# Query projection of two target blocks from f16 parts, with features at a quarter and the weight at four times

## The chip, the cores and the metric

One Trainium2 chip, one of its cores. The time is that of one execution of the whole program on the device, in microseconds (us); where a kernel was run several times the median stands. Engines are named as the profile names them: PE is the matrix engine (TensorE), PEld its weight loads, ACT the scalar engine, DVE the vector engine, POOL the GpSimd engine, SP the engine that issues DMAs.

## The reference

A graph attention layer. 2048 source nodes and 2048 target nodes have 256 features each; 8 heads of 32 features. What is computed, cut to the parts that matter:

```python
hs = layer_norm(h_source, ln1_scale, ln1_bias)
ht = layer_norm(h_target, ln1_scale, ln1_bias)
q = (ht @ Wq + bq).reshape(T, H, HD) / sqrt(HD)
k = (hs @ Wk + bk).reshape(S, H, HD)
v = (hs @ Wv + bv).reshape(S, H, HD)
logits = einsum('thd,shd->hts', q, k)            # masked where edge_mask is 0
ctx = einsum('hts,shd->thd', softmax(logits), v)
ht = layer_norm(ht + ctx @ Wo + bo, ln2_scale, ln2_bias)
return x + ht + gelu(ht @ W1) @ W2
```

The source rows are the rectified, normalized x; the edge mask is the adjacency matrix of 2048 x 2048 integers.

## The kernel before

Targets are worked in four blocks (k = 0 to 3) of 512. Within a block there are 8 units, one for each head (unit u = 8k + r), and within a unit 16 steps, one for each tile of 128 sources. (r, s) below is step s of the unit r of its block.

In each step PE makes the masked scores of the tile that is five steps ahead (`scores`: four mask matmuls of 128 columns and one of 512), a half of an `early_scores` pair (512 columns, for the row maxima of a later unit) and the context of the present tile (eight matmuls of 65 columns). ACT takes the exponential of the scores into one of 8 slots. The low part of the probabilities (exact value minus its 16-bit high part) is made by POOL for 12 of the 16 tiles and by DVE for 4. DVE also takes the row maxima of each early pair, `maxima`. Two early banks alternate, so PE can write pair e only when the maxima of pair e - 2 are done; two score banks alternate, so PE can write the scores of tile n only when the exponential of tile n - 2 is done. At the start of a unit PE waits until ACT has written the row of maxima for its scores (`row_out`), and until ACT has copied the context of the unit before (`context_out`).

Everything else is put by hand between these steps, in the order of each engine's own loop: tables at the top of the file say at which (r, s) or (u, s) a piece is issued. A piece stands in its engine's queue and holds up what comes behind it. The tables that matter here:

- `QT_AT`: at (3, 5) and (3, 11) PE transposes the normalized targets of the next block, and one step later ACT turns them into features (`query_features`) in `cT`, in f32.
- `QP_AT`: at (4, 1), (4, 2) and again at (4, 11), (4, 12) PE makes the queries of the next block, `queries(k, m, c)`: for each half m of the query columns one f32 product of 512 columns for each half c of the features. The trace shows each f32 product as two matmul records. The result is read by ACT (`query_high`) two steps after the start and by DVE (`query_low`) three steps after.
- `T_HIGH`, `T_LOW`: the same features are split into two f16 parts, high by ACT (`feature_high`), low by POOL (`feature_low`), for the residual term of the output rows (`out_row`), where an identity matrix `ident16` adds them. For the next block they stand at (4, 6), (4, 8) on ACT and (4, 11), (4, 14) on POOL.
- `MASK_DVE`: six of eight masks of the next block made by DVE, the last at (4, 7), where the second number counts pairs of steps.
- `HIGH_AT`, `LOW_AT`: W1 and W2 are split into f16 parts in eight pieces each, the high ones by ACT at step 6 of units 3, 4, 5, 6, 7, 12, 13, 14, the low ones by POOL (`weight_low`) at step 12 of units 4, 5, 6, 7, 13, 14, 15, 21.
- `WO_HIGH`, `WO_LOW`: the same for Wo, at (3, 2) on ACT and (4, 5) on POOL (`output_low`), both in block 0.
- At step (4, 1) of blocks 1 and up ACT takes a square root (`row_deviation`), which needs another activation table, and then goes back to the exponential's.

After the last unit comes the feed-forward part: PE makes `up_products` for 8 pieces of each block, ACT takes the gelu of each (`gelus`), DVE the low part, and PE makes `down_products`. The first gelu needs its own activation table.

Of the kernel before, what the change touches and what calls it, by code (L numbers as in the profile page):

```python
# [13 lines left out]
P = 128  # L14
# [6 lines left out]
DC = D // P  # L21
# [25 lines left out]
PLACE = 3 * 16  # L47


WIDE, UNREAD, UNREAD_LATER = 64, 20, 24  # L50
# [14 lines left out]

MASK_DVE = {(2, 3): 1, (2, 6): 2, (3, 2): 3, (3, 7): 4, (4, 3): 5, (4, 7): 6}

# [26 lines left out]
HIGH_AT = [3, 4, 5, 6, 7, 12, 13, 14]  # L94
LOW_AT = [4, 5, 6, 7, 13, 14, 15, 21]

# [98 lines left out]
def gnn_kernel(nc, x, adj, nodemask, h_target, ln1_scale, ln1_bias, Wq, bq, Wk, bk, Wv, bv, Wo, bo,  # L195
               ln2_scale, ln2_bias, W1, W2, out):
    with ExitStack() as top:
# [29 lines left out]
        nidentb = sb("nidentb", [P, P], BF16)  # L227
        ident16 = sb("ident16", [P, P], F16)
        ones16 = sb("ones16", [P, P], F16)
# [7 lines left out]
        node_b = sb("node_b", [P, NT], BF16)  # L237
        cols = sb("cols", [P, 10, DC], F32)
        big = sb("big", [P, 3], F32)
# [10 lines left out]

        LN1_G, LN1_B, BK, BQ, BO, BV, LN2_G, LN2_B, RES_B, Q_B = (cols[:, i, :] for i in range(10))
        std_z, rstd_z, neg_z, neg_x = (col_z[:, i, :] for i in range(4))
# [81 lines left out]
        q_hi = sem("q_hi")  # L334
        t_hi, t_lo, c_hi, c_lo, wo_hi, wo_lo = sem("t_hi"), sem("t_lo"), sem("c_hi"), sem("c_lo"), sem("wo_hi"), sem("wo_lo")
        w_in, w_hi, w_lo = [sem(f"w_in{i}") for i in range(2)], sem("w_hi"), sem("w_lo")
# [63 lines left out]
        with nc.Block() as block:  # L400
# [111 lines left out]
            def _(pe):  # L512
# [134 lines left out]
                def shift_row(u):  # L647
                    pe.wait_ge(shift_ready, u + 1)
                    if u == 0:

                        value_read(pe, 5)
                    aux_free(("shift", u))
                    for t in range(TT):
                        last = mm(aux[0:SHIFT_ROW + 1, t * P:(t + 1) * P], shift[:, t, :], ident16[:, :], True, True)
                    last.then_inc(aux_ready, 1)
# [16 lines left out]
                def out_row(k, t):  # L672

                    if t % 2 == 0:
                        aux_free(("wo", k, t // 2))
                    if t == 0:
                        pe.wait_ge(wo_lo, 1)
                        pe.wait_ge(c_lo, DC * (k + 1))
                        pe.wait_ge(t_lo, DC * (k + 1))
                    dst = aux[:, t % 2 * D:(t % 2 + 1) * D]  # L680
                    part = slice(t * P, (t + 1) * P)
                    for c in range(DC):
                        for a, w in ((0, 0), (0, 1), (1, 0)):
                            mm(dst, c_parts[:, a, c, part], wo_parts[:, w, c, :], c == a == w == 0, False, skip_group_check=True)
                    for c in range(DC):
                        for a in range(2):
                            last = mm(dst[:, c * P:(c + 1) * P], t_parts[k % 2][:, a, c, part], ident16[:, :], False,
                                      c == DC - 1 and a == 1, skip_group_check=True)
                    if t % 2 == 1:
                        last.then_inc(aux_ready, 1)  # L690
# [174 lines left out]
            def _(act):  # L865
# [84 lines left out]
                def negated(u):  # L950
                    act.wait_ge(max_done, (u + 1) * PAIRS)
                    if u > 0:

                        act.wait_ge(aux_ready, AUX["shift", u - 1] + 1)
                    else:
                        act.wait_ge(zeroed, 2)
                    nc.scalar.activation(shift[:, :, SHIFT_ROW], half_max[:, u % 2, 1, :], ACT.Copy, scale=-1.0).then_inc(
                        shift_ready, 1)
# [64 lines left out]
                def query_features(k, c):  # L1023
                    job_here("qT", k, c)
                    affine(t_full[k][:, c, :], aux[:, :], LN1_G[:, c:c + 1], RES_B[:, c:c + 1]).then_inc(aux_done, 1)

                def feature_high(k, c):
                    if k == 0:
                        act.wait_ge(nT_done, c + 1)
                    else:  # L1030
                        act.wait_ge(aux_done, AUX["qT", k, c] + 1)
# [97 lines left out]
                for u in range(UNITS):  # L1129
                    k, r = divmod(u, H)  # L1130
                    for s in range(STEPS):
# [10 lines left out]
                        if k == 0 and (r, s) in T_HIGH[0]:  # L1142
                            feature_high(0, T_HIGH[0].index((r, s)))
                        if k + 1 < NTB and (r, s) in T_HIGH[1]:
                            feature_high(k + 1, T_HIGH[1].index((r, s)))
                        if (u, s) == WO_HIGH:
# [375 lines left out]
            def _(pool):  # L1522
# [51 lines left out]
                def weight_low(i):  # L1574
# [20 lines left out]
                nc.gpsimd.memset(dead_w[:, :], DEAD_W).then_inc(made, 1)  # L1595
                for m in (ident32, identb, nidentb, ident16):
                    last = nc.gpsimd.memset(m[:, :], 0.0)
                link(last)
                for m, one in ((identb, 1.0), (ident32, 1.0), (nidentb, -1.0), (ident16, 1.0)):
                    last = nc.gpsimd.affine_select(out=m[:, :], in_=m[:, :], compare_op=ALU.not_equal, fill=one, base=0,  # L1600
# [22 lines left out]
                for u in range(UNITS):  # L1623
                    k, r = divmod(u, H)
                    for m in range(STEPS):
# [6 lines left out]
                        if k == 0 and (r, m) in T_LOW[0]:  # L1632
                            feature_low(0, T_LOW[0].index((r, m)))
                        if k + 1 < NTB and (r, m) in T_LOW[1]:
                            feature_low(k + 1, T_LOW[1].index((r, m)))
                        if k > 0 and (r, m) in C_LOW:
                            context_low(k - 1, C_LOW.index((r, m)))
                        if (u, m) == WO_LOW:
                            output_low()
                        if m == 12 and u in LOW_AT:  # L1640
                            weight_low(LOW_AT.index(u))

# [41 lines left out]
```

## Time and profile before

| what | us |
|---|---|
| median of 3 runs | 683.53 |
| lowest and highest of the 3 | 681.89, 683.69 |
| the profiled execution's own time | 682.28 |
| its span in the trace | 680.3 |
| the 32 units, from about | 66 to 582 |
| feed-forward part, from about | 582 to 680 |

The profiled execution is one more run of the same kernel; its span starts with the first instruction and leaves out 2.0 us around it. Every row of the trace is from this execution. In the timeline views a row is one instruction or several of the same kind merged, with start, duration, engine, line of the kernel, what it writes and reads, how many, and in brackets how long its engine stood idle before it and who ended that. The granted clock of PE was 1.00 in all of the units quoted, which is 2.4 GHz.

### The profile page before, as it was taken

To read this page: it belongs to the slowest core of one execution; us is meant where nothing else is said; L and a number is where in the kernel's file an instruction comes from. 1 tells how busy PE (TensorE), PEld (TensorE's weight loads), DVE (VectorE), ACT (ScalarE), POOL (GpSimd) and SP (SyncE) were. 2 spreads that over 40 slices of the span, in tenths; PEclk is the share of its full clock that TensorE was granted. 3 is DMA by queue.
4 is the path that set the end of the run, shared out by engine and by line. 5 is a ranking of instruction groups with operands and counts; after the bars stand their busy time and mean duration, and the time that the engine had idled before them with its cause. 6 is when DMAs were issued, how large, how long until landed. Compare 5 with 4: busy or idle time off the path is not lost. (4 is left out here: it accounts for less than half of the span.)

```text
span 680.3 us, 20543 instructions
## 1 busy us (share of the span) xinstructions
PE 649.9 (96%) x8402; PEld 464.2 (68%) x8402; DVE 567.2 (83%) x940; ACT 501.5 (74%) x973; POOL 542.4 (80%) x508
## 2 busy tenths in 40 slices
PE   4999999999999999999999999999999999899998
PEld 4556677766777777677777766777777667457767
DVE  5989899999989979888988798899878887595561
ACT  4767687777789858787898686877976788877450
POOL 4565889999999967999999679999997777383430
PEclk9999999999999999999999999999999999999999
DMA  8835512212101011220011112011000000000001
GB/s 290 281 91 151 167 33 64 64 50 63 33 2 34 2 65 63 67 76 2 2 33 33 64 55 57 19 67 59 4 2 1 2 2 2 1 1 32 24 18 54
DMA packets 20797, 36.23 MB, mean 53 GB/s; under 512 B 2752, under 2 KB 13280, under 8 KB 20704
## 3 DMA queue, kind: packets, MB, share of 16 engines
q1 hardware_dynamic: 20704, 34.92, 16.5%
q8 instruction: 66, 1.08, 0.7%
q14 instruction: 27, 0.22, 0.1%
HBM read 26.49 MB, written 2.10 MB: 42 GB/s over the span
## 5 line engine op out<-in xcount | busy, mean ns | idle before, releaser
L1532 POOL TENSOR_TENSOR prob_lo<-prob 128x512 f16<-128x512 f32 x379 | 432.5, 1168 | 45.7 <-ACT prob L945 44.7
L945 ACT ACTIVATE prob<-score 128x512 f32<-128x512 f32 x512 | 303.8, 597 | 110.4 <-PE score L514 102.5
L514 PE MATMUL score<-nidentb,mask_nat 128*128 128x128 bf16 x2048 | 198.3, 219 | 4.2 <-ACT prob L945 1.6
L514 PEld LDWEIGHTS ctx<-v_sb,prob 128*128 128x128 bf16 x2048 | 158.8, 98 | 61.9 <-ACT raw L967 13.8
L514 PE MATMUL early<-kT,qT 96*128 96x512 f16 x512 | 191.8, 380 | 6.7 <-DVE half_max L1316 5.7
L514 PE MATMUL score<-qT,kT 97*128 97x512 f16 x512 | 195.3, 381 | 0.0
L514 PE MATMUL ctx<-v_sb,prob 128*128 128x65 f16 x2048 | 191.5, 193 | 2.9 <-ACT raw L967 2.5
L1316 DVE CUSTOM_DVE_ANT_0 early<-early,mask_nat,half_max 128x1024 f32<-128x1024 f32 x128 | 163.9, 1286 | 33.3 <-PE early L514 31.7
L514 PE MATMUL ctx<-v_sb,prob_lo 128*128 128x65 f16 x2048 | 190.4, 193 | 0.0
L514 PEld LDWEIGHTS ctx<-v_sb,prob_lo 128*128 128x128 f16 x2048 | 142.6, 97 | 49.7 <-issue 4.0
L1316 DVE CUSTOM_DVE_ANT_0 early<-early,mask_nat 128x1024 f32<-128x1024 f32 x128 | 157.0, 1229 | 19.3 <-PE early L514 16.6
L1324 DVE TENSOR_TENSOR prob_lo<-prob 128x512 f16<-128x512 f32 x133 | 133.7, 1006 | 4.1 <-ACT prob L945 4.0
L514 PEld LDWEIGHTS score<-nidentb,mask_nat 128*128 128x128 bf16 x2048 | 121.5, 97 | 9.9 <-ACT prob L945 4.3
L514 PEld LDWEIGHTS early<-kT,qT 96*128 96x128 f16 x512 | 50.3, 99 | 17.5 <-DVE half_max L1316 13.3
L514 PEld LDWEIGHTS score<-qT,kT 97*128 97x128 f16 x512 | 50.1, 98 | 0.0
L514 PE MATMUL early<-w_f,kT 128*128 128x256 f16 x384 | 42.8, 273 | 1.1 <-DVE adj_in L1484 1.1
L1461 DVE TENSOR_TENSOR kT<-qT,kT 128x512 f16<-128x512 f32 x32 | 28.0, 885 | 17.7 <-ACT kT L1193 17.5
L514 PEld LDWEIGHTS early<-w_f,kT 128*128 128x128 f16 x384 | 37.4, 98 | 6.6 <-DVE adj_in L1484 1.7
L1660 POOL TENSOR_TENSOR mask_nat<-mask_nat,tgt 128x256 f32<-128x256 f32 x16 | 16.5, 1039 | 27.4 <-DVE mask_nat L1475 27.4
L1316 DVE DVE_READ_ACCUMULATOR2_ANT half_max<- 128x1 f32 x256 | 35.4, 138 | 0.0
L1189 ACT ACTIVATE qT<-score 128x512 f32<-128x512 f32 x32 | 19.0, 592 | 17.0 <-PE score L514 12.2
L983 ACT ACTIVATE q_stage<-raw,rden 128x32 f32<-128x32 f32 x96 | 25.3, 316 | 0.2
(185 smaller groups left out, 650.7 us busy)
## 6 DMA issues: line engine op xcount, KB each, us to landing
adj_in<-in_adj SPq DMA_DIRECT2D x26, 512.0 KB, 3.9
qT<-q_stage SPq DMA_DIRECT2D x48, 64.0 KB, 2.0
kT<-mask_nat SPq DMA_DIRECT2D x48, 64.0 KB, 2.0
raw<-in_x SPq DMA_DIRECT2D x4, 512.0 KB, 5.4
tgt<-in_L_gnn_h_target SPq DMA_DIRECT2D x4, 512.0 KB, 11.3
prob<-in_adj SPq DMA_DIRECT2D x4, 512.0 KB, 10.1
nT<-in_L_gnn_W SPq DMA_DIRECT2D x2, 1024.0 KB, 6.2
mask_nat<-in_x SPq DMA_DIRECT2D x1, 2048.0 KB, 9.7
```

The lines of the kernel that those rows point to most:

```text
L514: return nc.tensor.matmul(dst, w, m, start=start, stop=stop, **more)
L945: nc.scalar.activation(prob[:, n % SLOTS, :], score[n % 2][:, :], ACT.Exp).then_inc(exp_done, 1)
L983: last = nc.scalar.activation(cnorm[:, t, h * HD:(h + 1) * HD], raw_of(k)[:, t, h, 0:HD], ACT.Copy, scale=rden[:, t * H + h:t * H + h + 1])
L1189: nc.scalar.activation(gelu[:, f % 2, :], up[f % 2][:, :], ACT.Gelu_apprx_tanh).then_inc(gelu_ready, 1)
L1316: nc.vector.tensor_tensor_reduce(out=early[e % 2][:, :], in0=early[e % 2][:, :], in1=mask_nat[:, k % 2, t, half * HALF:(half + 1) * HALF], ...
L1324: nc.vector.tensor_tensor(prob_lo[:, n % SLOTS, :], prob[:, n % SLOTS, :], prob_hi(n % SLOTS), ALU.subtract).then_inc(lo_sem["dve"], 1)
L1461: nc.vector.tensor_tensor(g_lo[:, k % 2, f, :], gelu[:, f % 2, :], g_hi[:, k % 2, f, :], ALU.subtract).then_inc(g_lo_done, 1)
L1532: nc.gpsimd.tensor_tensor(prob_lo[:, n % SLOTS, :], prob[:, n % SLOTS, :], prob_hi(n % SLOTS), ALU.subtract).then_inc(lo_sem["pool"], 1)
L1660: nc.gpsimd.tensor_tensor(xin[:, n - 1, :], xin[:, n - 1, :], tgt[:, n - 1, :], ALU.add).then_inc(r_done, 1)
```

## The change

- The targets' features that go through `cT` are kept at a quarter of their value (`LN1_GQ`, `RES_BQ`: scale and bias times 0.25, made by ACT once), and Wq at four times (`query_weights_four`, ACT, once, at unit 1 step 10). The product is the same. Block 0's own features are multiplied by 0.25 after use (`first_quarter`, ACT, at (2, 9) and (2, 11) of block 0). The f16 identity becomes `quad16`, with 4 on its diagonal, so that the residual term is as before; the row of maxima is scaled with -0.25 for the same reason.
- Wq is split into two f16 parts in the memory of Wo: high by ACT at unit 6 step 9, low by POOL at unit 11 step 1.
- The queries of blocks 2 and 3 are made from the f16 parts of features and weight, three f16 products (high with high, low weight with high, high weight with low) in place of each f32 one. Block 1's stay f32. PE now waits for all the feature parts and for the weight's parts before the first of them.
- For blocks 2 and 3 the parts are therefore made earlier: ACT at (3, 7), (3, 13) instead of (4, 6), (4, 8); POOL at (3, 12), (4, 2) instead of (4, 11), (4, 14).
- The eight `weight_low` pieces on POOL move to units 11, 19 and 20. The last DVE mask of each block moves from (4, 7) to (4, 6).
- Before the last `context_out` ACT runs a gelu on one column, which brings the loading of the gelu table ahead of it.

```diff
-MASK_DVE = {..., (4, 3): 5, (4, 7): 6}
+MASK_DVE = {..., (4, 3): 5, (4, 6): 6}
-T_HIGH = {0: [(3, 7), (3, 9)], 1: [(4, 6), (4, 8)]}
-T_LOW = {0: [(3, 12), (3, 15)], 1: [(4, 11), (4, 14)]}
+T_HIGH = {0: [(3, 7), (3, 9)], 1: [(4, 6), (4, 8)], 2: [(3, 7), (3, 13)], 3: [(3, 7), (3, 13)]}
+T_LOW = {0: [(3, 12), (3, 15)], 1: [(4, 11), (4, 14)], 2: [(3, 12), (4, 2)], 3: [(3, 12), (4, 2)]}
+T_QUARTER = [(2, 9), (2, 11)]
+WQ_FOUR, WQ_HIGH, WQ_LOW = (1, 10), (6, 9), (11, 1)
-LOW_AT = [4, 5, 6, 7, 13, 14, 15, 21]
+LOW_AT = [(11, 3), (11, 8), (11, 13), (19, 3), (19, 8), (19, 13), (20, 2), (20, 7)]
...
+        wq_parts = wo[:, :, :].rearrange("p c n -> p (c n)").bitcast(F16).rearrange("p (r c n) -> p r c n", r=2, c=DC)
...
                 def queries(k, m, c):
                     if c == 0:
                         aux_free(("qp", k, m))
-                    last = mm(aux[:, :], wq[:, c, m * P:(m + 1) * P], t_full[k][:, c, :], c == 0, c == DC - 1)
+                        pe.wait_ge(wq_four, 1)
+                        if k > 1:
+                            pe.wait_ge(t_lo, DC * (k + 1))
+                            pe.wait_ge(wq_lo, 1)
+                    if k == 1:
+                        last = mm(aux[:, :], wq[:, c, m * P:(m + 1) * P], t_full[k][:, c, :], c == 0, c == DC - 1)
+                    else:
+                        for i, (w, a) in enumerate(((0, 0), (1, 0), (0, 1))):
+                            last = mm(aux[:, :], wq_parts[:, w, c, m * P:(m + 1) * P], t_parts[k % 2][:, a, c, :], c == i == 0,
+                                      c == DC - 1 and i == 2)
...
+                def quarter_columns():
+                    act.wait_ge(res_b, 1)
+                    for q, full in ((LN1_GQ, LN1_G), (RES_BQ, RES_B)):
+                        nc.scalar.activation(q, full, ACT.Copy, scale=QUARTER).then_inc(quarters, 1)
+                def query_weights_four():
+                    act.wait_ge(kq_ready, DC)
+                    nc.scalar.activation(wq[:, :, :], wq[:, :, :], ACT.Copy, scale=1.0 / QUARTER).then_inc(wq_four, 1)
+                def query_weights_high():
+                    act.wait_ge(wo_lo, 1)
+                    act.wait_ge(wq_four, 1)
+                    nc.scalar.activation(wq_parts[:, 0, :, :], wq[:, :, :], ACT.Copy).then_inc(wq_hi, 1)
+                def first_quarter(c):
+                    act.wait_ge(nT_done, c + 1)
+                    nc.scalar.activation(t_full[0][:, c, :], t_full[0][:, c, :], ACT.Copy, scale=QUARTER).then_inc(quarters, 1)
...
+                nc.scalar.activation(warm_c, eps_c, ACT.Gelu_apprx_tanh).then_inc(act_link, 1)
                 context_out(UNITS - 1)
...
+                def query_weights_low():
+                    pool.wait_ge(wq_hi, 1)
+                    nc.gpsimd.tensor_tensor(wq_parts[:, 1, :, :], wq[:, :, :], wq_parts[:, 0, :, :], ALU.subtract).then_inc(wq_lo, 1)
```

## Rows read from the trace of the kernel before

**Rows 1.** The page's head: span; busy time, share and instructions of each engine.
```profile
span 680.3 us, 20543 instructions
PE 649.9 (96%) x8402; PEld 464.2 (68%) x8402; DVE 567.2 (83%) x940; ACT 501.5 (74%) x973; POOL 542.4 (80%) x508
```
**Rows 2.** Busy time by stretch, units 11 and 12: stretch, its length, engines, clock, DMA.
```profile
245.11:262.63 17.52, 17.22 (x256) 13.38 (x256) 14.27 (x27) 11.96 (x23) 12.75 (x13) 1.00 0.18 59
262.63:281.54 18.91, 18.73 (x241) 12.43 (x239) 16.97 (x29) 15.53 (x29) 15.66 (x17) 1.00 0.18 58
```
**Rows 3.** Groups by line: busy us, mean ns of one, idle before.
```profile
L514 PE MATMUL aux<-cT,wq 128*128 128x512 f32 x24 | 12.3, 591 | 0.0
...
L1587 POOL TENSOR_TENSOR nTq<-cT,nTq 128x512 f16<-128x512 f32 x6 | 7.8, 1304 | 0.0
...
L1578 POOL TENSOR_TENSOR w_f<-nT,w_f 128x512 f16<-128x512 f32 x8 | 9.2, 1155 | 0.0
...
L1582 POOL TENSOR_TENSOR wo_parts<-wo,wo_parts 128x512 f16<-128x512 f32 x1 | 1.6, 1606 | 0.0
...
L1042 ACT ACTIVATE wo_parts<-wo 128x512 f16<-128x512 f32 x1 | 0.6, 622 | 0.0
...
L957 ACT ACTIVATE shift<-half_max 128x4 f16<-128x4 f32 x32 | 6.8, 213 | 0.7 <-DVE half_max L1316 0.7
```
**Rows 4.** PE's timeline around both query jobs of unit 12.
```profile
264.00 1.02 PE L514 MATMUL aux<-cT,wq 128*128 128x512 f32 x2
265.10 0.38 PE L514 MATMUL score<-nidentb,mask_nat 128*128 128x128 bf16 x4
...
265.74 0.39 PE L514 MATMUL early<-kT,qT 96*128 96x512 f16 x1
...
268.15 0.40 PE L514 MATMUL score<-nidentb,mask_nat 128*128 128x128 bf16 x4
...
275.66 1.02 PE L514 MATMUL aux<-cT,wq 128*128 128x512 f32 x2
```
**Rows 5.** ACT's timeline of unit 12: the table loads, and the second feature part.
```profile
264.59 1.28 ACT L1006 ACT_TABLE_LOAD   x1
...
267.50 1.08 ACT L945 ACTIVATE prob<-score 128x512 f32<-128x512 f32 x2
...
273.19 0.64 ACT L1039 ACTIVATE nTq<-cT 128x512 f16<-128x512 f32 x1
```
**Rows 6.** DVE's timeline of units 12 and 13: masks, and maxima after the second query job.
```profile
265.54 0.68 DVE L1304 TENSOR_SCALAR mask_nat<-adj_in 128x1024 bf16<-128x1024 int32 x1
...
279.52 1.29 DVE L1316 CUSTOM_DVE_ANT_0 early<-early,mask_nat,half_max 128x1024 f32<-128x1024 f32 x1 [1.83 <-PE early L514]
...
283.19 1.32 DVE L1304 TENSOR_SCALAR mask_nat<-adj_in 128x1024 bf16<-128x1024 int32 x1
```
**Rows 7.** PE's timeline of unit 13: a wait for maxima.
```profile
285.83 0.39 PE L514 MATMUL early<-kT,qT 96*128 96x512 f16 x1 [0.28 <-DVE half_max L1316]
```
**Rows 8.** POOL's timeline from the start of unit 11 into unit 12.
```profile
243.84 3.30 POOL L1532 TENSOR_TENSOR prob_lo<-prob 128x512 f16<-128x512 f32 x3 [2.04 <-ACT prob L945]
...
258.00 3.48 POOL L1532 TENSOR_TENSOR prob_lo<-prob 128x512 f16<-128x512 f32 x3 [0.64 <-ACT prob L945]
261.83 3.48 POOL L1532 TENSOR_TENSOR prob_lo<-prob 128x512 f16<-128x512 f32 x3 [0.34 <-ACT prob L945]
```
**Rows 9.** ACT's timeline where `first_quarter` is put, unit 2.
```profile
107.93 0.59 ACT L962 ACTIVATE qT<-aux 1x512 f16<-1x512 f32 x1
...
109.53 1.20 ACT L945 ACTIVATE prob<-score 128x512 f32<-128x512 f32 x2
```
**Rows 10.** PE's timeline at the start of the feed-forward part.
```profile
581.74 4.05 PE L514 MATMUL score<-nTq,w_f 128*128 128x512 f16 x18
```
**Rows 11.** ACT's timeline at the same place.
```profile
582.35 1.28 ACT L1189 ACT_TABLE_LOAD   x1
...
588.00 0.60 ACT L1189 ACTIVATE qT<-score 128x512 f32<-128x512 f32 x1 [0.79 <-PE score L514]
```

More of the change, by code:

```diff
@@ L47 @@
 PLACE = 3 * 16
+QUARTER = 0.25
 WIDE, UNREAD, UNREAD_LATER = 64, 20, 24
@@ L227, in gnn_kernel @@
         nidentb = sb("nidentb", [P, P], BF16)
-        ident16 = sb("ident16", [P, P], F16)
+        quad16 = sb("quad16", [P, P], F16)
         ones16 = sb("ones16", [P, P], F16)
@@ L237, in gnn_kernel @@
         node_b = sb("node_b", [P, NT], BF16)
-        cols = sb("cols", [P, 10, DC], F32)
+        cols = sb("cols", [P, 12, DC], F32)
         big = sb("big", [P, 3], F32)
@@ L249, in gnn_kernel @@
         col_l = sb("col_l", [P, 2, 2 * TT], F32)
-        LN1_G, LN1_B, BK, BQ, BO, BV, LN2_G, LN2_B, RES_B, Q_B = (cols[:, i, :] for i in range(10))
+        LN1_G, LN1_B, BK, BQ, BO, BV, LN2_G, LN2_B, RES_B, Q_B, LN1_GQ, RES_BQ = (cols[:, i, :] for i in range(12))
         std_z, rstd_z, neg_z, neg_x = (col_z[:, i, :] for i in range(4))
@@ L334, in gnn_kernel @@
         q_hi = sem("q_hi")
-        t_hi, t_lo, c_hi, c_lo, wo_hi, wo_lo = sem("t_hi"), sem("t_lo"), sem("c_hi"), sem("c_lo"), sem("wo_hi"), sem("wo_lo")
+        t_hi, t_lo, c_hi, c_lo, wo_hi, wo_lo, quarters, wq_four, wq_hi, wq_lo = sem("t_hi"), sem("t_lo"), sem("c_hi"), sem("c_lo"), sem("wo_hi"), sem("wo_lo"), sem("quarters"), sem("wq_four"), sem("wq_hi"), sem("wq_lo")
         w_in, w_hi, w_lo = [sem(f"w_in{i}") for i in range(2)], sem("w_hi"), sem("w_lo")
@@ L653, in shift_row @@
                     for t in range(TT):
-                        last = mm(aux[0:SHIFT_ROW + 1, t * P:(t + 1) * P], shift[:, t, :], ident16[:, :], True, True)
+                        last = mm(aux[0:SHIFT_ROW + 1, t * P:(t + 1) * P], shift[:, t, :], quad16[:, :], True, True)
                     last.then_inc(aux_ready, 1)
@@ L686, in out_row @@
                         for a in range(2):
-                            last = mm(dst[:, c * P:(c + 1) * P], t_parts[k % 2][:, a, c, part], ident16[:, :], False,
+                            last = mm(dst[:, c * P:(c + 1) * P], t_parts[k % 2][:, a, c, part], quad16[:, :], False,
                                       c == DC - 1 and a == 1, skip_group_check=True)
@@ L956, in negated @@
                         act.wait_ge(zeroed, 2)
-                    nc.scalar.activation(shift[:, :, SHIFT_ROW], half_max[:, u % 2, 1, :], ACT.Copy, scale=-1.0).then_inc(
+                    nc.scalar.activation(shift[:, :, SHIFT_ROW], half_max[:, u % 2, 1, :], ACT.Copy, scale=-QUARTER).then_inc(
                         shift_ready, 1)
@@ L1024, in query_features @@
                     job_here("qT", k, c)
[L1025 removed]
+                    act.wait_ge(quarters, 2)
+                    affine(t_full[k][:, c, :], aux[:, :], LN1_GQ[:, c:c + 1], RES_BQ[:, c:c + 1]).then_inc(aux_done, 1)
+                def quarter_columns():
[12 more added lines that the diff above has]
+                    nc.scalar.activation(t_full[0][:, c, :], t_full[0][:, c, :], ACT.Copy, scale=QUARTER).then_inc(quarters, 1)
                 def feature_high(k, c):
                     if k == 0:
[L1029 removed]
+                        act.wait_ge(quarters, 2 + c + 1)
                     else:
@@ L1143, in _ @@
                             feature_high(0, T_HIGH[0].index((r, s)))
-                        if k + 1 < NTB and (r, s) in T_HIGH[1]:
-                            feature_high(k + 1, T_HIGH[1].index((r, s)))
+                        if k + 1 < NTB and (r, s) in T_HIGH[k + 1]:
+                            feature_high(k + 1, T_HIGH[k + 1].index((r, s)))
+                        if (u, s) == WQ_FOUR:
+                            quarter_columns()
+                            query_weights_four()
+                        if (u, s) == WQ_HIGH:
+                            query_weights_high()
+                        if k == 0 and (r, s) in T_QUARTER:
+                            first_quarter(T_QUARTER.index((r, s)))
                         if (u, s) == WO_HIGH:
@@ L1595, in _ @@
                 nc.gpsimd.memset(dead_w[:, :], DEAD_W).then_inc(made, 1)
-                for m in (ident32, identb, nidentb, ident16):
+                for m in (ident32, identb, nidentb, quad16):
                     last = nc.gpsimd.memset(m[:, :], 0.0)
                 link(last)
-                for m, one in ((identb, 1.0), (ident32, 1.0), (nidentb, -1.0), (ident16, 1.0)):
+                for m, one in ((identb, 1.0), (ident32, 1.0), (nidentb, -1.0), (quad16, 1.0 / QUARTER)):
                     last = nc.gpsimd.affine_select(out=m[:, :], in_=m[:, :], compare_op=ALU.not_equal, fill=one, base=0,
@@ L1633, in _ @@
                             feature_low(0, T_LOW[0].index((r, m)))
-                        if k + 1 < NTB and (r, m) in T_LOW[1]:
-                            feature_low(k + 1, T_LOW[1].index((r, m)))
+                        if k + 1 < NTB and (r, m) in T_LOW[k + 1]:
+                            feature_low(k + 1, T_LOW[k + 1].index((r, m)))
                         if k > 0 and (r, m) in C_LOW:
                             context_low(k - 1, C_LOW.index((r, m)))
+                        if (u, m) == WQ_LOW:
+                            query_weights_low()
                         if (u, m) == WO_LOW:
                             output_low()
-                        if m == 12 and u in LOW_AT:
-                            weight_low(LOW_AT.index(u))
+                        if (u, m) in LOW_AT:
+                            weight_low(LOW_AT.index((u, m)))
                 for t in range(TT):
```

2 lines of the change are left out of this document (1 added, 1 removed).

## The prediction, as put on record before the change was run

> **What bounds the kernel now.** I read the page's head first: PE is busy 96% of the span, DVE 83%, POOL 80%, ACT 74% [rows 1]. PE is the engine to watch, but a share over the whole span does not say whether a saving in one step lasts. So I went to the two units that the change works on, by stretch [rows 2]. In unit 12, where queries are made, PE is busy 18.73 of 18.91 us, and DVE 16.97 us. The reader should see that PE fills the unit and that DVE is close behind. Then I read PE's timeline around the query jobs and asked after each for the next matmul that does not start when PE is free but when another engine lets it. That place is what a faster query is measured against. If PE stands there anyway, the time saved ahead of it is only longer waiting.
>
> **The query matmuls.** The 24 f32 records last 591 ns each but overlap [rows 3]; what PE gives is the distance of starts. A pair of them spans 1.02 us, which less the 0.16 us that a 512-column matmul runs past its successor's start is 0.86 us [rows 4]. Three f16 products take their place. At the start of the feed-forward part 18 such matmuls span 4.05 us, (4.05 - 0.16)/18 = 0.216 us each [rows 10], so three are 0.65 us. A replaced product saves 0.21 us. There are 2 blocks x 2 jobs x 2 products = 8, or 1.7 us of PE's time in all. What of it lasts:
>
> The first job (products at 264.00 and 265.96) does not give it through. The exponential two tiles ahead of the scores at 268.15 starts at 267.50 and ends at 268.10, because ACT loads two tables from 264.59 on [rows 4, 5], and ACT came to them from an exponential whose scores PE made before the query began. PE is at those scores about 0.2 us early now, and would be 0.6 us early. It also stands 0.2 us ahead of the early scores at 265.74: the mask matmuls at 265.10 and the score matmul take 0.22 us each, so 265.54 would be its time [rows 4]. The saving of the first job, 0.42 us, goes into these waits: **0**, in both blocks (unit 20 repeats unit 12's pattern).
>
> The second job (from 275.66) does. After it DVE is idle 1.83 us until PE delivers the next early scores, and its maxima start at 279.52 [rows 6]. From there DVE works without a gap, and the next wait of PE, at 285.83, is for that chain [rows 7]. As the chain starts when PE lets it, it starts earlier by what PE saved. **-0.42 us** per block, -0.84 us in all.
>
> **Feature parts moved on ACT.** The two copies of 0.62 us leave steps (4, 6) and (4, 8). The second ran at 273.19, just ahead of the exponential and the row of maxima for which PE waits at the start of unit 13 [rows 5]. Between nothing and its 0.5 us of occupied time (0.64 less the 0.1 us by which ACT's instructions overlap) comes back there. I take -0.2 us for block 1. In block 2 no weight piece is on ACT beside it, so ACT is not behind; I take 0. At (3, 7) and (3, 13), in unit 11, ACT is busy 11.96 of 17.52 us over 16 steps, 0.35 us idle per step [rows 2], and a copy is caught up in two steps: 0.
>
> **POOL, and the new wait.** PE's wait for `t_lo` stands in its queue at (4, 1), ahead of the context of that step and all later scores; ACT's exponentials, then both low parts, wait for those. In unit 11 POOL is busy 12.75 of 17.52 us, and was idle 2.04 us just before it [rows 2, 8]: 6.8 us of room. The change puts in the low part of Wq (1.6 us, the price of the one of Wo), three `weight_low` of 1.155 us and the first `feature_low` of 1.3 us [rows 3], 6.4 us in all. The room is in pieces, so POOL becomes late: the low part that ended at 258.00 + 3.48 = 261.48 [rows 8] will end between 262.5 and 263.1, and the second `feature_low` behind it between 263.8 and 264.5. PE wants it at 264.00 [rows 4]. A wait of up to 0.5 us there comes before the two places where PE waits anyway, 0.4 us now and 0.8 us with the faster products. So it costs 0, as long as the low part is there by 264.8; behind that every tenth is lost. Context matmuls of the tiles around it were 1.6 to 3 us behind their low parts before and keep about 1 us. Unit 19 has the same load less the Wq part; in unit 20 two further pieces follow, and I leave 0 to +0.5 us for them, value +0.1. Taking pieces out of units 4 to 7, 13 to 15 and 21 frees POOL where PE did not wait for it: 0.
>
> **DVE.** The mask goes from behind the maxima of pair 7 to before them. The chain from 279.52 on holds the same instructions in another order, and PE's wait at 285.83 is for its end. The mask costs 0.68 us when it runs freely and 1.32 us otherwise [rows 6]. PE will wait up to 0.8 us one pair sooner and correspondingly less at the later one: 0, bounds -0.3 and +0.3 us for each of three blocks.
>
> **ACT in block 0.** A copy of 512 elements takes 0.62 us, 0.52 us of it unshared, and one of a few elements 0.21, 0.1 unshared [rows 3]. At (1, 10) come 0.72 us, at (2, 9) and (2, 11) twice 0.52 us, at (6, 9) 0.52 us. PE writes scores n when exponential n - 2 is done, and now stands about 0.3 us clear of that (an estimate, from ACT's idle time per step). The row of maxima at 107.93 is followed by the exponential at 108.55, and two more at 109.53 [rows 9]; with two copies and the two target rows between, they come 0.5 and 1.0 us later. By hand along this queue PE is held 0.46 us at the start of unit 3, of which 0.4 is taken up by waits for DVE and ACT that stand there anyway. At (1, 10) and (6, 9) I get 0.07 and 0.16 us. Together **+0.3 us**, bounds 0 and +1.0.
>
> **The gelu table.** The load of 1.28 us at 582.35 moves into ACT's idle time before it. But PE's 18 matmuls from 581.74 on are without a gap, and ACT stands 0.79 us idle at 588.00 waiting for PE [rows 10, 11]. The first gelu could come 0.4 us sooner (its product ends at about 583.2) and nothing follows: **0**, bounds -0.3 and 0. The Trainium skill, ScalarE: Activation LUTs, What ACT_TABLE_LOAD costs, gives 1283 ns for the load and about 1380 ns for draining; here the load is 1.28 us and the gelu begins right behind it, so the drain is not seen.
>
> **Sum.** -0.84 - 0.2 + 0.1 + 0.3 = -0.64 us. On the profiled execution: 682.28 - 0.64 = 681.6. The median of three runs stands 1.25 us above that execution; of all four the median is (682.28 + 683.53)/2 = 682.9. I take this as the base: 682.9 - 0.6 = **682.3 us**. 0.3% is 2.05 us; a measurement of this kernel can hardly tell less from no change.
>
> **Rivals.**
> *All of PE's saving lasts, and DVE's chain gets shorter.* For it: PE is busy 96%. If the waits at 268.15 were PE's own, 1.7 us would come; and a POOL freed of 2.6 us of feature parts in unit 12 could let DVE's masks and low parts run at 0.68 in place of 1.32 us, at two or three places a block. Against: the tables at 264.59. Price: -1.7 - 0.2 - 3 x 0.6 + 0.4 = -3.3 us, 679.6. Chance 0.18.
> *POOL and DVE hold each other in units 11 and 19.* DVE's mask at 265.54 took 0.68 us with POOL nearly idle and another 1.32 us beside POOL work [rows 6]. The change fills POOL where DVE is late already. Three DVE instructions at 0.64 us more make its maxima about 1.9 us late; 0.8 us is covered as above, so PE loses 1.1 us per block; with `feature_low` after 264.8 on top, 0.5 us more. It decides if POOL's lateness passes 0.8 us beyond 264.0. Price: 2 x 1.6 + 0.3 - 0.8 = +2.7 us, 685.6. Chance 0.13.
> The Trainium skill, SBUF — State Buffer, SBUF: two separate sides, says that VectorE and GpSimd share one port pair under an exclusive lock and the loser waits for the whole instruction. The two mask durations agree with it; it speaks for this second rival.
> *Nothing happens.* The f16 products wait where the f32 ones did, ACT's additions eat the rest: 682.9 to 683.5, part of the forecast's own range.
>
> **How the numbers follow.** Forecast (within -1.5 and +0.8 us) 0.69, first rival 0.18, second 0.13. The forecast's own range is 681.4 to 683.7 us. To hold 8 in 10, with half of each rival and 0.7 us by which repeated runs of this kernel differ: 680.4 to 684.7. The first rival is beyond 2.05 us in most of its cases, the second in somewhat over half: faster by over 0.3% 0.17, within 0.3% 0.74, slower 0.09.
>
> **What would show it.** Right: after the first query job PE waits longer at the counterpart of 268.15, and the start of unit 13, counted from the start of unit 12, comes about 0.5 us sooner; query records are f16, 12 per block, 0.216 us apart. ACT's table load lies ahead of the last context copy and the feed-forward part is as long as before. Wrong: PE's wait at (4, 1) for `t_lo` of over 0.8 us, PE waiting for POOL's low parts in units 11, 19 or 20, or DVE masks and low parts that are all short or all long there.

## The result, and the profile after

The changed kernel takes 683.31 us (median), the kernel before 682.03 us over as many runs: 1.0019 times as long, 95% interval 1.0013 to 1.0025. So it is slower by 1.3 us, where I had forecast 0.6 us faster. The median of before that I knew, 683.53 of three runs, had caught the upper end of its runs; the base of 682.9 that I took from four executions was still 0.9 us too high. I had also said that a measurement can hardly tell less than 0.3% from no change; over 20 runs of each the interval is 0.12% wide.

The head of the page of the changed kernel, which answers to [rows 1]:

```profile
span 681.5 us, 20584 instructions
## 1 busy us (share of the span) xinstructions
PE 648.8 (95%) x8410; PEld 463.6 (68%) x8410; DVE 564.5 (83%) x940; ACT 503.1 (74%) x980; POOL 541.7 (79%) x509
```

PE is busy 1.1 us less and the span is 1.2 us longer: PE saved work and stood longer. Shares do not say where. The units do. For this table I took from each trace the start of the first context matmul of every unit; the length of a unit is the distance to that of the next. Before is in us, the others as differences from it; units that differ nowhere by over 0.06 us are left out. The last column is the changed kernel with its weight pieces undone, the first experiment below.

```
unit        before   changed   pieces back
 2           15.27     +0.54      +0.56
 3           16.33     -0.12      -0.12
 5           16.43     +0.03      +0.14
 6           14.91     +0.37      +0.38
 7           14.90     +0.17       0.00
 8           15.37      0.00      +0.06
10           19.28     -0.08      -0.07
11           17.53     +0.82      +0.33
12           18.91     -0.60      -0.60
13           16.39     -0.49      -0.49
15           14.91     +0.17       0.00
16           15.47     -0.10      +0.01
19           17.53     +0.83      +0.33
20           18.72     +0.38      -0.42
21           16.54     -0.59      -0.62
whole span  680.32     +1.19      -0.34
```

All other units repeat to within 0.06 us from kernel to kernel, so a tenth can be read here, which a median cannot give. The part ahead of unit 0 (66.94 us before) does not repeat so well: it was 0.05 us shorter in the changed kernel and 0.14 us longer with the pieces back, where the two run the same code. So a whole span is known to about 0.2 us, a unit far better. Gains stand in unit 12, where queries are made, and in units 13 and 21 behind such units. The losses are 0.8 us each in units 11 and 19, 0.4 us in units 2 and 3 together, 0.4 us in unit 6, 0.17 us each in units 7 and 15, and 0.4 us in unit 20, where queries are made too.

First, what went as foreseen. PE's timeline of the changed kernel around the first query job of unit 12, beside [rows 4]:

```profile
265.67 0.81 PE L522 MATMUL aux<-nTq,wo 128*128 128x512 f16 x3
266.56 0.38 PE L522 MATMUL score<-nidentb,mask_nat 128*128 128x128 bf16 x4
...
269.82 0.40 PE L522 MATMUL score<-nidentb,mask_nat 128*128 128x128 bf16 x4 [0.40 <-ACT prob L962]
```

Three f16 products span 0.81 us, 0.65 us of PE's time. Behind the job PE now stands for ACT's exponential, where it was hardly held before: from 268.80 (early scores) to 269.82 lie 0.47 us of work and 0.55 us of waiting, against 0.19 us before. The saving of the first job is gone into that.

Then the place of the loss: DVE's timeline of unit 11, changed kernel.

```profile
254.19 1.06 DVE L1349 TENSOR_SCALAR mask_nat<-adj_in 128x1024 bf16<-128x1024 int32 x1
255.17 1.52 DVE L1369 TENSOR_TENSOR prob_lo<-prob 128x512 f16<-128x512 f32 x1
...
260.06 1.30 DVE L1369 TENSOR_TENSOR prob_lo<-prob 128x512 f16<-128x512 f32 x1
261.29 1.22 DVE L1361 CUSTOM_DVE_ANT_0 early<-early,mask_nat 128x1024 f32<-128x1024 f32 x1
```

And the same instructions in the kernel before:

```profile
253.33 0.69 DVE L1304 TENSOR_SCALAR mask_nat<-adj_in 128x1024 bf16<-128x1024 int32 x1
253.94 1.53 DVE L1324 TENSOR_TENSOR prob_lo<-prob 128x512 f16<-128x512 f32 x1
...
258.84 0.76 DVE L1324 TENSOR_TENSOR prob_lo<-prob 128x512 f16<-128x512 f32 x1
259.51 1.22 DVE L1316 CUSTOM_DVE_ANT_0 early<-early,mask_nat 128x1024 f32<-128x1024 f32 x1
```

The maxima (custom operation) keep their 1.22 us; the mask and the low part of tile 14 take 0.37 and 0.54 us longer. Why is read from POOL, changed kernel, and from PE, which pays:

```profile
252.54 1.16 POOL L1623 TENSOR_TENSOR w_f<-nT,w_f 128x512 f16<-128x512 f32 x1
253.66 3.93 POOL L1577 TENSOR_TENSOR prob_lo<-prob 128x512 f16<-128x512 f32 x3
...
258.67 1.04 POOL L1577 TENSOR_TENSOR prob_lo<-prob 128x512 f16<-128x512 f32 x1
259.67 1.15 POOL L1623 TENSOR_TENSOR w_f<-nT,w_f 128x512 f16<-128x512 f32 x1
260.78 3.48 POOL L1577 TENSOR_TENSOR prob_lo<-prob 128x512 f16<-128x512 f32 x3
...
264.22 1.15 POOL L1636 TENSOR_TENSOR nTq<-cT,nTq 128x512 f16<-128x512 f32 x1
```
```profile
262.62 0.39 PE L522 MATMUL early<-kT,qT 96*128 96x512 f16 x1 [0.46 <-DVE half_max L1361]
```

DVE starts its low part at 260.06, in the middle of the weight piece that runs until about 260.8; it ends 0.55 us after that. Before, the POOL instruction under way at 258.84 ended at about 259.05, and DVE's ended at 259.60. The mask is another case. At 254.19 no weight piece is under way but one of POOL's own low parts (253.66 to about 254.7), which the weight piece at 252.54 had made late. In the kernel before, the mask ran freely from 253.33, because POOL was idle until its next low part:

```profile
253.84 1.08 POOL L1532 TENSOR_TENSOR prob_lo<-prob 128x512 f16<-128x512 f32 x1 [1.11 <-ACT prob L945]
```

The spacing is the same throughout the traces. In the kernel before, 115 of DVE's 151 masks and low parts in the 32 units began while a POOL instruction was under way. 101 of them took over 0.70 us, and each of these ended 0.55 us after that POOL instruction, to 0.01 us. So DVE's instruction takes what is left of POOL's, and then 0.55 us. The maxima behind it are later by that, and PE waits for them at 262.62. It is not the number of such meetings that counts: over the whole kernel DVE's low parts took even less than before, 129.8 us against 133.7 us. The last row of POOL also shows the new wait in PE's queue to be harmless: the feature part ends at 265.37, the query begins at 265.67.

### The profile page after: what moved, and what is told of

It reads as the page before. It is cut to its first block and busy times, and to the rows that moved or that the text cites. A ratio compares the mean times of both kernels' runs of the same rounds, so it can differ in the third digit from the quotient of the medians.

```text
span 681.5 us, 20584 instructions
## 1 busy us (share of the span) xinstructions
PE 648.8 (95%) x8410; PEld 463.6 (68%) x8410; DVE 564.5 (83%) x940; ACT 503.1 (74%) x980; POOL 541.7 (79%) x509
## 5 line engine op out<-in xcount | busy, mean ns | idle before, releaser
L1369 DVE TENSOR_TENSOR prob_lo<-prob 128x512 f16<-128x512 f32 x133 | 129.8, 977 | 4.1 <-ACT prob L962 4.0
```

The source lines that it names most:

```text
L1369: nc.vector.tensor_tensor(prob_lo[:, n % SLOTS, :], prob[:, n % SLOTS, :], prob_hi(n % SLOTS), ALU.subtract).then_inc(lo_sem["dve"], 1)
```

## The experiments

Each was timed beside the kernel before on the same chip (its medians there were 682.0 to 682.3 us), and each left a trace. Between chips medians of before thus differ by 0.2 us, so experiments are best compared by their distance to before, or by units.

**e1_low_back: the weight pieces back.**

```diff
-LOW_AT = [(11, 3), (11, 8), (11, 13), (19, 3), (19, 8), (19, 13), (20, 2), (20, 7)]
+LOW_AT = [(4, 12), (5, 12), (6, 12), (7, 12), (13, 12), (14, 12), (15, 12), (21, 12)]
```

> The changed kernel with one part undone: the eight low weight pieces on POOL are back at their places of before (step 12 of units 4 to 7, 13 to 15, 21). If those pieces are what delays units 11, 19 and 20 (by +0.8, +0.8 and +0.4 us in the changed kernel), the three units give back 1.5 to 2 us and the kernel ends at about 681.6, a little under the kernel before; DVE's mask of unit 11 takes 0.7 us again. If the moved feature parts or the new wait of PE do it, it stays within 0.3 us of the changed kernel, 683.3.

Measured: 681.61 us, 0.9986 of before (0.9977 to 0.9996). That is 1.7 us under the changed kernel, and 0.6 us under before on the same chip. The table's last column shows where: 0.5 us each from units 11 and 19, 0.8 us from unit 20, 0.17 us each from units 7 and 15. Against that units 5 and 16 lost 0.1 us each. The move of the pieces was the largest single loss. Units 11 and 19 keep 0.33 us. DVE's timeline of unit 11 of this kernel:

```profile
254.43 0.69 DVE L1349 TENSOR_SCALAR mask_nat<-adj_in 128x1024 bf16<-128x1024 int32 x1
...
259.93 1.19 DVE L1369 TENSOR_TENSOR prob_lo<-prob 128x512 f16<-128x512 f32 x1
```

The mask runs freely again, 0.37 us less than in the changed kernel; the low part of tile 14 takes 0.11 us less. Together that is the unit's 0.49 us, to a hundredth. So most of what the pieces cost here came from POOL's own low parts, which they had made late, and little from a weight piece under DVE's instruction. In unit 20 of the changed kernel no mask or low part of DVE began under a weight piece at all. There it was POOL's low parts again that held DVE up, a low part of DVE for 1.32 us (0.68 us with the pieces back) and an operation on four columns for 1.02 us (0.13 us):

```profile
401.21 1.32 DVE L1369 TENSOR_TENSOR prob_lo<-prob 128x512 f16<-128x512 f32 x1
...
405.55 1.02 DVE L1416 TENSOR_SCALAR col_l<-mv_l 128x4 f32<-128x4 f32 x1
```

**e2_no_quarter: without the scaling.** `QUARTER` is 1, and `quarter_columns`, `query_weights_four`, `first_quarter` and the waits for them are left out.

```diff
-                        if (u, s) == WQ_FOUR:
-                            quarter_columns()
-                            query_weights_four()
...
-                        if k == 0 and (r, s) in T_QUARTER:
-                            first_quarter(T_QUARTER.index((r, s)))
```

> The changed kernel without the scaling: features and weight stay at their full value, so ACT's two small copies, the copy of Wq and the two copies of block 0's features are left out; the result is the same up to how far the low f16 parts reach. If ACT's additions in unit 2 cause the first 0.5 us of loss, the time falls by 0.4 to 0.6 us, to 682.8, and unit 2 takes 15.3 us instead of 15.8. My own sum had 0.1 us for it. The 0.4 us in unit 6 stays, since the high part of Wq is still made there.

Measured: 683.24 us, 1.0012 of before (1.0003 to 1.0021). That is 0.1 us under the changed kernel's median, but that one was timed beside a before of 682.03 us and this one beside 682.25 us: against before it is 1.0 us slower where the changed kernel is 1.3 us slower. The trace is plainer: unit 2 took 15.27 us instead of 15.81, unit 3 16.34 instead of 16.21, and every other unit what it took in the changed kernel, a gain of 0.41 us. The expectation held in the units; the times alone, 0.3 us apart, leave it open. ACT's timeline of the changed kernel at (2, 9), beside [rows 9]:

```profile
107.88 0.59 ACT L979 ACTIVATE qT<-aux 1x512 f16<-1x512 f32 x1
108.50 0.63 ACT L1061 ACTIVATE nTq<-nTq 128x512 f32<-128x512 f32 x1
109.15 0.60 ACT L962 ACTIVATE prob<-score 128x512 f32<-128x512 f32 x1
...
110.61 0.63 ACT L1061 ACTIVATE nTq<-nTq 128x512 f32<-128x512 f32 x1
111.13 1.08 ACT L962 ACTIVATE prob<-score 128x512 f32<-128x512 f32 x2
```

The first copy displaces the exponential by 0.65 us, not by the 0.52 us of my sum; the second, the same instruction with the same kind of wait ahead of it, displaces the next by 0.52 us. Why the overlap of 0.1 us is missing at the first, no run shows.

**e3_f32_queries: the products alone.**

```diff
-                    if k == 1:
+                    if k >= 1:
                         last = mm(aux[:, :], wq[:, c, m * P:(m + 1) * P], t_full[k][:, c, :], c == 0, c == DC - 1)
```

> The changed kernel with the queries of blocks 2 and 3 from f32 products again, all waits and moved parts kept; it prices the f16 products alone. If only the second job of each block gives its saving through, it is 0.8 us slower than the changed kernel (684.1). If all of PE's saving lasts, 1.7 us (685.0). If none does, no difference.

Measured: 684.34 us, 1.0 us over the changed kernel (0.8 us, if each is taken against before on its own chip). Unit 12 took 18.73 us where the changed kernel took 18.31, unit 20 19.52 where it took 19.10: 0.42 us each. No other unit differed from the changed kernel by more than 0.04 us. PE's saving is 0.86 us in each block, and half of it arrives. With the f32 products unit 12 is still 0.18 us shorter than before. That is the size I had forecast for ACT without the two feature copies; POOL's two parts left the unit as well, and no run separates them.

**e4_mask_back: the mask at its old place.**

```diff
-MASK_DVE = {(2, 3): 1, (2, 6): 2, (3, 2): 3, (3, 7): 4, (4, 3): 5, (4, 6): 6}
+MASK_DVE = {(2, 3): 1, (2, 6): 2, (3, 2): 3, (3, 7): 4, (4, 3): 5, (4, 7): 6}
```

> The changed kernel with the last DVE mask of each block back at pair 7 instead of pair 6. The order within DVE's chain changes, not its length: within 0.3 us of the changed kernel. If the earlier mask is what removed PE's waits at the start of units 13 and 21 (0.5 and 0.6 us shorter in the changed kernel than before), those units lengthen by that and the time rises by up to 1.5 us over three blocks.

Measured: 686.17 us, 2.9 us over the changed kernel. Units 5, 13 and 21 were longer than in it by 0.82, 0.91 and 0.87 us, nothing else changed. The second expectation held: an order of DVE that I had priced at nothing was holding off 2.6 us. DVE's timeline of this kernel in unit 5:

```profile
148.22 0.75 DVE L1374 SCALAR_TENSOR_TENSOR q_stage<-aux,cols,q_stage 128x512 f16<-128x512 f32 x1
148.88 1.56 DVE L1369 TENSOR_TENSOR prob_lo<-prob 128x512 f16<-128x512 f32 x1
...
151.57 1.32 DVE L1349 TENSOR_SCALAR mask_nat<-adj_in 128x1024 bf16<-128x1024 int32 x1
...
154.01 1.32 DVE L1369 TENSOR_TENSOR prob_lo<-prob 128x512 f16<-128x512 f32 x1
...
157.64 0.84 DVE L1369 TENSOR_TENSOR prob_lo<-prob 128x512 f16<-128x512 f32 x1
```

And of the changed kernel:

```profile
148.19 1.24 DVE L1349 TENSOR_SCALAR mask_nat<-adj_in 128x1024 bf16<-128x1024 int32 x1
149.35 0.74 DVE L1374 SCALAR_TENSOR_TENSOR q_stage<-aux,cols,q_stage 128x512 f16<-128x512 f32 x1
150.01 0.86 DVE L1369 TENSOR_TENSOR prob_lo<-prob 128x512 f16<-128x512 f32 x1
...
153.20 1.11 DVE L1369 TENSOR_TENSOR prob_lo<-prob 128x512 f16<-128x512 f32 x1
...
156.62 0.68 DVE L1369 TENSOR_TENSOR prob_lo<-prob 128x512 f16<-128x512 f32 x1
```

In the kernel before, which has the old order too, the first of these low parts took only 0.71 us:

```profile
148.47 0.71 DVE L1324 TENSOR_TENSOR prob_lo<-prob 128x512 f16<-128x512 f32 x1
```

Here it took 1.56 us, 0.85 us more, and unit 5 is longer than before by just that (17.28 against 16.43 us). It hangs on very little: POOL's row of low parts had begun 1.87 us ahead of DVE's instruction before, 2.01 us ahead here, and at that distance a POOL instruction has just ended and the next just begun.

The same four instructions (one mask, three low parts) take 1.56 + 1.32 + 1.32 + 0.84 = 5.04 us in the one order and 1.24 + 0.86 + 1.11 + 0.68 = 3.89 us in the other. The difference is 1.15 us, while the instructions are the same: it is how far a POOL instruction had got when each of them came.

**e9_before_mask: that move alone.** The kernel before, with `(4, 7): 6` as `(4, 6): 6` in `MASK_DVE`.

> The kernel before with one part of the change alone: the last DVE mask of each block at pair 6 instead of pair 7. In the changed kernel that move is worth 0.8 to 0.9 us in each of units 5, 13 and 21. If it is worth that by itself, this is 2.5 us faster than before, 679.5. If its worth comes from how DVE and POOL meet in the changed kernel, it is within 1 us of before, either way.

Measured: 682.77 us, 1.0010 of before (1.0001 to 1.0020). Units 5, 8, 13 and 21 were longer by 0.16, 0.11, 0.14 and 0.16 us. So the move gains nothing by itself, and the changed kernel without it was 3.9 us slower than before (e4_mask_back). It is worth something only where the other parts have shifted POOL against DVE, as in unit 5 above. With the weight pieces at their old places, as in the last two kernels below, the mask's old place was not tried; units 5 and 8 are 0.16 and 0.09 us longer there than before, as here.

**e8_memset: POOL's time without its reads.** The low pieces as in e1_low_back, and at the eight places of the changed kernel:

```diff
+                        if (u, m) in PROBE_AT:
+                            pool.wait_ge(wq_lo, 1)
+                            for _ in range(2):
+                                link(nc.gpsimd.memset(wq[:, :, :], 0.0))
```

> The kernel e1_low_back (low weight pieces at their old places), and at the eight places in units 11, 19 and 20 where the changed kernel has them POOL writes zeros instead, twice 512 columns into Wq's f32 memory, which nothing reads any more there; about 1.1 us each, as long as a piece, but reading nothing. The output is unaffected. If the pieces cost PE time because POOL's reads keep DVE's masks and low parts waiting, this stays within 0.3 us of e1_low_back (681.6), and DVE's mask at the end of unit 10's row of pairs in unit 11 stays near 0.7 us. If they cost because POOL itself gets late, it is about as slow as the changed kernel (683.3).

Measured: 682.13 us, between the two. Units 11 and 19 took 17.78 us, 0.08 us less than in e1_low_back and 0.57 us less than in the changed kernel. Unit 20 took 18.92 us, 0.62 us of the 0.80 us that the pieces cost it. DVE's timeline of unit 11 of this kernel:

```profile
254.17 1.12 DVE L1350 TENSOR_SCALAR mask_nat<-adj_in 128x1024 bf16<-128x1024 int32 x1
...
260.10 0.66 DVE L1370 TENSOR_TENSOR prob_lo<-prob 128x512 f16<-128x512 f32 x1
```

My expectation of the mask was wrong: it took 1.12 us. The fill in front had made POOL's own low part of a tile late, so that it ran into the mask, as the weight piece does in the changed kernel. The mask is 0.43 us longer than in e1_low_back, the low part of tile 14 is 0.53 us shorter (0.66 against 1.19 us), and the sum of the two, -0.10 us, is about the unit's -0.08 us. So the fills did no less harm at the mask than the pieces; a lucky meeting at tile 14 made up for it.

The run does not show what it was made for, that DVE is free beside a POOL instruction which only writes. The two fills at that place are two instructions of 0.53 us:

```profile
259.69 1.11 POOL L1695 MEMSET wq<- 128x512 f32 x2
```

The first had 0.11 us left when DVE came, and low parts of DVE that come with 0.11 us left of a reading POOL instruction take 0.68 to 0.69 us, hardly more than the 0.66 us here. What it does show is the other direction. The second fill began 0.17 us into DVE's low part and took 0.53 us, like all sixteen fills. In e11_best_tlow below, a feature part of POOL, which reads, began 0.17 us into the same low part of DVE and took 1.61 us, where such a part takes 1.15 us when DVE leaves it alone:

```profile
259.32 1.61 POOL L1636 TENSOR_TENSOR nTq<-cT,nTq 128x512 f16<-128x512 f32 x1
```

In unit 20 the shift lengthened a low part of DVE to 1.54 us, and PE then stood 0.55 us for the maxima. So in all three units a large part of the harm is POOL's lateness: fills, which read nothing, do it too.

**e6_low_late: the pieces elsewhere.**

```diff
-LOW_AT = [(11, 3), (11, 8), (11, 13), (19, 3), (19, 8), (19, 13), (20, 2), (20, 7)]
+LOW_AT = [(15, 12), (23, 4), (23, 12), (24, 12), (28, 3), (28, 8), (28, 13), (30, 12)]
```

> The changed kernel with the low weight pieces at (15, 12), (23, 4), (23, 12), (24, 12), (28, 3), (28, 8), (28, 13), (30, 12), in units where DVE is not a bound. Like e1_low_back it should lose the 1.8 us of units 11, 19 and 20: 681.5 to 681.9. If it is only the number of POOL reads in any unit, units 23, 24 and 28 lengthen instead and it stays near 683.

Measured: 683.84 us. Units 11, 19 and 20 were as in e1_low_back to 0.01 us. But unit 24 was longer by 0.87 us, 29 by 0.48 us and 31 by 0.95 us. I had looked for units in which DVE has room and not asked for POOL's. In unit 24 PE now waits 0.7 us for a low part of POOL itself, and in the last unit twice, 1.5 us in all, where it had waited 0.5 us before. In unit 29 the new wait of PE is one of 0.24 us for a low part of DVE. The waits of the last unit:

```profile
PE ctx L522 <- POOL prob_lo L1577: 1.5, 2, 0.8
```

**e7_late_and_act: the ACT copies elsewhere as well.** On top of e6_low_late:

```diff
-T_QUARTER = [(2, 9), (2, 11)]
-WQ_FOUR, WQ_HIGH, WQ_LOW = (1, 10), (6, 9), (11, 1)
+T_QUARTER = [(2, 1), (2, 3)]
+WQ_FOUR, WQ_HIGH, WQ_LOW = (1, 10), (6, 12), (11, 1)
```

> e6_low_late, and on ACT block 0's two quartering copies at (2, 1) and (2, 3) instead of (2, 9) and (2, 11), the high part of Wq at unit 6 step 12 instead of 9. If the 0.5 us in unit 2 and the 0.4 us in unit 6 come from ACT having these copies beside the row of maxima and the target rows, both go: 0.7 to 0.8 us below e6_low_late, about 680.9. If ACT's time counts wherever it is put, no difference.

Measured: 683.04 us, 0.8 us under e6_low_late. Units 2, 3 and 6 took their lengths of before (15.27, 16.33 and 14.91 us). The same copies, none of them fewer, cost nothing eight steps earlier (block 0's features) or three steps later (the weight).

**e10_best: what paid, kept.** e1_low_back with the edit of e7_late_and_act.

> The changed kernel with the low weight pieces at their places of before, block 0's quartering copies at (2, 1) and (2, 3), and the high part of Wq at unit 6 step 12: the parts that paid are kept, the three that cost are undone. By the units it should be e1_low_back less 0.4 us of units 2 and 3 and 0.4 us of unit 6: 680.8, about 1.2 us (0.17%) faster than the kernel before. If the costs only move elsewhere, as the late pieces did, it stays at 681.6.

Measured: 680.68 us, 0.9983 of before (0.9974 to 0.9992), as expected: 1.36 us faster.

**e11_best_tlow: one POOL instruction three steps on.** On top of e10_best:

```diff
-T_LOW = {..., 2: [(3, 12), (4, 2)], 3: [(3, 12), (4, 2)]}
+T_LOW = {..., 2: [(3, 15), (4, 2)], 3: [(3, 15), (4, 2)]}
```

> e10_best with the first low feature part of blocks 2 and 3 at (3, 15) instead of (3, 12). Units 11 and 19 are still 0.33 us longer than before. If that is this POOL piece holding up DVE's low part of tile 14, both go back to 17.5 us and 0.6 us is gained, 680.2. If moving it only meets the next DVE instruction, or makes PE wait for the parts in units 12 and 20, no gain or a loss of some tenths.

Measured: 679.99 us, 0.9968 of before (0.9956 to 0.9980): 2.05 us faster, and the best of all kernels here. Units 11 and 19 took 17.53 us, as before the change. DVE's low part of tile 14 of unit 11 took 1.19 us in e1_low_back, which has this part where e10_best has it. Here:

```profile
259.15 0.75 DVE L1369 TENSOR_TENSOR prob_lo<-prob 128x512 f16<-128x512 f32 x1
```

What had held it up was again not the moved part itself but a low part of POOL behind it. The moved part now meets DVE's last low part of the unit, which takes 1.25 us; that costs nothing, for it took 1.39 us there in the kernel before.

## Why the prediction was wrong

The sign was wrong: -0.64 us forecast, +1.2 us in the span. The step that failed is the POOL term, +0.1 us in the sum. Point by point, by the steps of the sum:

- **The query matmuls: right.** Predicted -0.42 us per block from the second job and nothing from the first; e3_f32_queries gives 0.42 us in unit 12 and 0.42 us in unit 20. The first job's part went mostly into the wait behind the table loads, 0.19 us before, 0.55 us after.
- **Feature parts moved on ACT: right in size.** Predicted -0.2 us in block 1 and 0 in block 2. e3_f32_queries shows unit 12 0.18 us shorter than before, and in e1_low_back unit 20 is 0.42 us shorter, which the products alone account for. That it is ACT's copies, and not POOL's parts, is argued and not shown.
- **The new wait of PE: right.** Predicted free; the feature part ended at 265.37 and PE came to it at 265.67, both later than I had them (264.5 and 264.0).
- **The gelu table: right.** The load came at 581.29, in ACT's idle time; the part behind the last context matmul took 98.57 us instead of 98.61 us.
- **POOL: the step that failed.** I weighed POOL's room as time (6.4 us of work into 6.8 us of idle time) and asked only when its results are needed. By that measure all of it cost +0.1 us. The pieces cost 1.7 us (e1_low_back) and the place of the first feature part another 0.66 us (e11_best_tlow, units 11 and 19), 2.4 us in all. The reason is that every piece moves POOL's own low parts against DVE, and DVE is held up until the POOL instruction under way has ended. The second rival had POOL and DVE holding each other up, and the two durations of the mask in [rows 6] were in front of me; I gave it 0.13. Its price of 1.1 us per block was near what the pieces and the feature part cost together in unit 11 (0.82 us, with units 19 and 20 at 0.83 and 0.80 us). The chance was wrong, not the rival: I had taken the two durations as luck that averages out, where in this kernel every unit repeats to a few hundredths.
- **Freed units of POOL: 0 predicted, +0.1 us found.** Units 7 and 15 lost 0.17 us each when their piece went, units 5 and 16 won 0.1 us. Taking POOL work away can make PE wait longer. In the units before, 6 and 14, DVE's low part of tile 14 took 1.55 and 1.54 us instead of the 0.69 and 1.07 us of e1_low_back; that this is what PE pays for a unit later, I have not followed step by step.
- **DVE's mask: 0 predicted, bounds 0.3 us a block.** By itself +0.4 us in all (e9_before_mask), and 2.6 us saved in the changed kernel (e4_mask_back). "The same instructions in another order" was the second false step: the sum of their durations depends on the order. This term also hid how much the rest had cost. The terms as measured, -0.84 - 0.2 + 2.4 + 0.8 (the next one) = +2.2 us, lie 1.0 us above the +1.2 us of the span. About that much stands as a gain in units 13 and 21 (-0.49 and -0.59 us), which became losses of 0.42 and 0.28 us when the mask went back.
- **ACT in block 0: right in kind, too small.** +0.3 us predicted, +0.42 us in units 2 and 3 and +0.37 us in unit 6, total 0.8 us, within its bounds of 0 and 1.0. Of the two copies in unit 2 one displaces 0.65 us, not 0.52 us. And of what the copies cost there I let waits behind swallow 0.4 us; of the 0.54 us they took 0.12 us (unit 3). Unit 1 cost nothing, where I had 0.07 us, and unit 6 cost 0.37 us, where I had 0.16 us.
- **The base.** I took 682.9 us; twenty runs gave 682.03 us. The forecast's 682.3 us would have been 681.4 us from there.

The Trainium skill, SBUF — State Buffer, SBUF: two separate sides, says that the shared port pair goes to whoever starts first for a whole instruction, and that a VectorE operation with two SBUF inputs is concerned only against a GpSimd operation that reads. The traces agree with the first part: DVE's low parts end 0.55 us after the POOL instruction that they found under way. For the second part there is one direction only: the fill of e8_memset that began under a low part of DVE was not held up (0.53 us), a feature part that reads was (1.61 instead of 1.15 us). Whether a fill holds DVE up, no run here shows.

With the four costly placements changed (weight pieces, quartering copies, the high part of Wq, the first low feature part) and the products kept, the change is worth 2.05 us. What was slow about it was where its helpers stood.

## What to carry to other kernels

When VectorE is close to being a bound, do not price GpSimd work by its idle time: look at each VectorE instruction near the new place that reads SBUF alone, as the masks and low parts here do, and ask which GpSimd instruction will be halfway through when it comes. Here it was mostly not the new one but an old one that the new one had displaced. In a kernel that repeats its schedule to hundredths, such meetings are not noise: 0.14 us of shift was worth 0.85 us in one unit, and the same instruction three steps on was free. A probe that stands in for another instruction must have its length in one piece; my two short fills in place of one long instruction left its main question open. And compare units of two traces rather than totals: an edit that gains 0.9 us and one that loses it both vanish in the sum, and only taking one part back at a time showed that the smallest edit of this change was holding off 2.6 us.

## What I had not expected of the hardware

A mask or low part on DVE takes 0.68 to 0.69 us when no POOL instruction is under way, and up to 1.57 us when one of 1.04 us has just begun: the rest of POOL's instruction plus 0.55 us. It works the other way too: a low part of POOL, 1.04 us otherwise, takes up to 1.58 us when one of DVE has just begun. DVE's maxima, which read the scores and one mask, stay at 1.20 to 1.29 us whatever POOL does. A loss of POOL work made PE's units longer, by 0.17 us in units 7 and 15.
